# Mixture of experts: expert results added up by token in DRAM instead of stored, gathered and combined; four tiles fed by one-hot products; rows turned in mid-tile

## The reference, cut to what matters

```python
def _L0_ffn_ref(x, keys, w1, b1, w2, b2, rw, rb):
    # 512 tokens, D = 256, E = 16 experts, TOP_K = 4, F = 1024
    logits = -dist2 + jnp.einsum('bld,ed->ble', x, rw) + rb
    topv, topi = jax.lax.top_k(logits, TOP_K)
    w = jax.nn.softmax(topv, axis=-1)
    hidden = jax.nn.gelu(jnp.einsum('bld,efd->blef', x, w1) + b1, approximate=False)
    exp_out = jnp.einsum('blef,edf->bled', hidden, w2) + b2
    sel = jnp.take_along_axis(exp_out, topi[..., None], axis=2)
    return jnp.sum(w[..., None] * sel, axis=2)
...
x = x + _L0_ffn_ref(_layernorm(x, axis=-1), ...)
x = x + _L1_xattn_ref(_layernorm(x, axis=-1), ctx_1024, ctx_1024, mask, gamma, beta)
```

## Time and profile before

| | us |
|---|---|
| time, median of 3 runs | 872.52 |
| the runs | 868.11 to 873.1 |
| profiled execution, time | 865.21 |
| profiled execution, span | 863.3 |
| TensorE busy in the span | 723.3 (84%) |
| DVE busy | 501.6 (58%) |
| POOL busy | 313.4 (36%) |

### The profile page before, as it was taken

One profiled execution on the slowest core, in us unless ns is written; L12 is line 12 of the kernel. 1 busy time (PEld: TensorE's weight loads), 2 busy tenths in 40 slices (PEclk: granted clock), 3 DMA queues, 4 the chain that ended last, 5 costly groups with the idle time before them and its releaser, 6 DMA issues.

```text
span 863.3 us, 13603 instructions
## 1 busy us (share of the span) xinstructions
PE 723.3 (84%) x4928; PEld 550.0 (64%) x4928; DVE 501.6 (58%) x830; ACT 387.6 (45%) x729; POOL 313.4 (36%) x365
## 2 busy tenths in 40 slices
PE   5899999999999749699999999946976866665686
PEld 2677777777778538599999999932532322222575
DVE  4787778878778674011111111116666989997675
ACT  3766656656655323234444444412257643331441
POOL 6545425525445105540000000034103657753330
PEclk9999999999999958899999999987997999999898
DMA  7201101011002396898878888858210000000210
GB/s 313 75 2 49 32 19 49 0 49 49 0 0 98 131 412 253 287 354 305 311 293 310 304 310 309 320 205 347 98 55 0 0 1 0 0 0 0 74 36 25
DMA packets 19073, 118.18 MB, mean 137 GB/s; under 512 B 2144, under 2 KB 6768, under 8 KB 11728
## 3 DMA queue, kind: packets, MB, share of 16 engines
q1 hardware_dynamic: 16000, 109.28, 34.0%
q0 software_dynamic: 3024, 8.26, 2.5%
HBM read 106.79 MB, written 10.75 MB: 136 GB/s over the span
## 4 chain that ended last, share of the span: by engine, by line
PE 54%; DVE 24%; issue 8%; ACT 5%; POOL 4%; DMA 3%; DVEq 0%; SPq 0%; ACTq 0%; POOLq 0%; PEldq 0%
PE banks L1659 48%; DVE banks L1554 8%; PE banks L1721 4%; DVE k_stack L1154 3%; POOL x_slots L740 2%; ACT k_stack L850 1%; DVE negmax_raw L1206 1%; DVE hid_lo L1615 1%; DVE X L1622 1%; DVE shown L1562 1%; ACT ctx_hi L842 1%; DMA first<-in_first 1%; DVE conv L1279 1%; POOL y_rows L760 1%; DMA y_rows<-y_slots,slots 1%
## 5 line engine op out<-in xcount | busy, mean ns | idle before, releaser
L932 ACT ACTIVATE mid<-banks,later 128x128 f32<-128x128 f32 x248 | 91.1, 368 | 150.6 <-PE banks L1659 150.5
L1659 PEld LDWEIGHTS banks<-xT,raw 128*128 128x128 f32 x992 | 147.9, 192 | 12.2 <-issue 1.1
L1659 PE MATMUL banks<-xT,raw 128*128 128x128 f32 x992 | 151.6, 276 | 0.6 <-DVE xT L1389 0.6
L1659 PE MATMUL banks<-raw,mid 128*128 128x256 f32 x496 | 148.3, 382 | 0.0
L1395 DVE COPY y_tile<-banks 128x256 f32<-128x256 f32 x31 | 13.2, 424 | 197.6 <-PE banks L1659 197.6
L792 POOL TENSOR_TENSOR inject<-Bbc,drive 128x1024 f32<-128x1024 f32 x32 | 75.3, 2356 | 66.9 <-DVE banks L1554 29.9
L863 ACT ACTIVATE probs<-banks,negmax 128x1024 f32<-128x1024 f32 x64 | 71.5, 1117 | 58.4 <-DVE negmax L1209 57.7
L1659 PE MATMUL banks<-shown,table 128*128 128x512 f32 x128 | 66.4, 644 | 36.6 <-DVE shown L1562 29.9
L1206 DVE TENSOR_REDUCE negmax_raw<-banks 128x1 f32<-128x1024 f32 x64 | 78.0, 1218 | 20.5 <-PE banks L1659 20.5
L755 POOL DMA_DIRECT2D y_slots<-y_tile x31 | 17.0, 547 | 190.0 <-DVE y_tile L1395 189.9
L1659 PEld LDWEIGHTS banks<-raw,mid 128*128 128x128 f32 x496 | 75.8, 193 | 0.1
(11 more groups left out here) (285 smaller groups left out, 1399.4 us busy)
## 6 DMA issues: line engine op xcount, KB each, us to landing
raw<-in_w SPq DMA_DIRECT2D x31, 2048.0 KB, 8.7
ctx_raw<-in_ctxT SPq DMA_DIRECT2D x8, 1024.0 KB, 4.8
ctxT<-in_ctxT SPq DMA_DIRECT2D x4, 2048.0 KB, 8.4
ctxN<-in_ctxN SPq DMA_DIRECT2D x4, 2048.0 KB, 8.6
x_slots<-zero SPq DMA_DIRECT2D x1, 3968.0 KB, 12.5
y_slots<-y_tile POOLq DMA_DIRECT2D x31, 128.0 KB, 7.3
wf<-in_w SPq DMA_DIRECT2D x9, 384.0 KB, 3.0
later<-in_later SPq DMA_DIRECT2D x1, 2646.0 KB, 16.0
```

Of the source, the lines that this page charges most:

```text
L932: nc.scalar.activation(mid[n % HB][:], pb(UP_BANKS[n % 3])[:, 0:P], ACT.Gelu, bias=b1[:, bass.ds(at + u, 1)]).then_inc(gelu_done, 1)
L1659: return nc.tensor.matmul(o, lhsT, rhs, start=start, stop=stop)
```

## The change

What it removes: the stores to y_slots, the 16 gathers, the 16 combining steps, the product of gates and choices.

What it adds:
- A scattered row is 17 floats wider (XW = 273, 1,092 bytes): it carries the token's number, less an offset, and the token's 16 gates. The tile x_ext takes the place of xn for this layer. The gates are therefore computed inside place_rows, ahead of the slots.
- DVE reads from the arrived rows which token each row belongs to (tokens_of; unused rows go to a spare row behind the tokens) and its gate (gate_at). The first four tiles have their rows from the one-hot product, and for them a small load (hot_meta, 4 x 128 pieces of 68 bytes) fetches these 17 floats. In overflow tiles the gate is picked by the owner (owner_hot, over_gate). All of it happens on DVE at i = 3, between take_rows(4) and take_tile(3), after waits for all three pieces.
- take_tile multiplies by the gate as it evicts. Tiles 0 to 2 are evicted without it and weighed in place later (weigh_tile).
- GpSimd adds each y_tile by an indirect DMA with an add into x_added in DRAM, 640 rows of 256 floats, zeroed before. One add is issued when the one before has landed. take_tile(i) waits until add i - 4 has landed.
- After the last add SP loads x_added as four tiles of 128 KB, and DVE adds them to X. The layer norms then follow for all four tiles, and the attention starts after them. The two next context loads no longer wait for gathers.
- HOT is 4, so one more tile is fed by the one-hot product, and X_PIECES is (4, 8, 16, 31).
- turn_rows(i+1) comes in the middle of tile i, at its fifth unit, not at its start.

The core of the diff:

```diff
-HOT = 3
-X_PIECES = (HOT, HOT + 4, 16, TILES)
+HOT = 4
+X_PIECES = (HOT, HOT + 4, E0, TILES)
+XW, Z_PARTS = D + 1 + E0, 13
...
+            half = (TOK + P) * D // P // 2
+            sp.dma_start(x_added.rearrange("(p a) n -> p (a n)", p=P).rearrange("p (k n) -> p k n", k=2), over(zero[:, 0:half], 2, 1))\
                 .then_inc(zeroed, 16)
...
+                if k == 1:
+                    sp.dma_start(hot_meta[:], by_row[:, 0:HOT, D:XW]).then_inc(rows_loaded[1], 16)
+                sp.dma_start(x_rows[:, a - HOT:b - HOT, :], by_row[:, a:b, :]).then_inc(rows_loaded[k], 16)
...
-            sp.wait_ge(gathered[0], 16 * TOP0)
+            sp.wait_ge(y_added, 16 * TILES)
+            for t in range(TC):
+                sp.dma_start(x_sum[:, t, :], x_added[t * P:(t + 1) * P, :]).then_inc(gathered[t], 16)
             context_T(2)
             context_N(2)
-            sp.wait_ge(gathered[1], 16 * TOP0)
             context_T(3)
...
-            pool.wait_ge(zeroed, 16)
+            pool.wait_ge(zeroed, 32)
             pool.wait_ge(slots_ready, 1)
+            pool.wait_ge(gate_ready, 1)
...
-            def store_tile(i):
-                pool.wait_ge(y_taken, i + 1)
-                pool.dma_start(y_slots[i * P:(i + 1) * P, :], y_tile[i % YB][:]).then_inc(y_stored[i % YB], 16)
...
+            def add_rows(i):
+                if i < HOT - 1:
+                    pool.wait_ge(y_weighed, i + 1)
+                else:
+                    pool.wait_ge(y_taken, i + 1)
+                if i:
+                    pool.wait_ge(y_added, 16 * i)
+                nc.gpsimd.indirect_dma_start(x_added, bass.IndirectOffsetOnAxis(token[:, i:i + 1], 0), y_tile[i % YB][:], None,
+                                             compute_op=ALU.add).then_inc(y_added, 16)
...
+            order.step(nc.vector.tensor_reduce(here[:], earlier[:, 0:P], AX.X, ALU.add))
+            order.step(nc.vector.tensor_scalar(here[:], here[:], -1.0, float(P - 1), ALU.mult, ALU.add))
+            order.step(nc.vector.tensor_scalar(x_ext[:, :, D], inc[:, 0:TC], float(P), -float(TOK + P), ALU.mult, ALU.add))
+            order.mark(nc.vector.tensor_scalar(x_ext[:, :, D], x_ext[:, :, D], here[:], None, ALU.add))
...
                 one_hot(0)
+                gates()
...
+            def tokens_of(tiles, found):
+                order.step(nc.vector.tensor_scalar(spare[:, tiles], found, 0.0, here[:], ALU.is_equal, ALU.mult))
+                order.step(nc.vector.scalar_tensor_tensor(token_f[:, tiles], found, float(TOK), spare[:, tiles], ALU.add, ALU.add))
+                order.step(nc.vector.tensor_copy(token[:, tiles], token_f[:, tiles]))
+
+            def rows_arrive(k):
+                if k == 1:
+                    dve.wait_ge(rows_loaded[1], 32)
+                    tokens_of(slice(0, HOT), hot_meta[:, :, 0])
+                else:
+                    dve.wait_ge(rows_loaded[k], 16)
+                a, b = X_PIECES[k], X_PIECES[k + 1]
+                tokens_of(slice(a, b), x_rows[:, a - HOT:b - HOT, D])
+                if k == 2:
+                    order.step(nc.vector.tensor_tensor(owner_hot[:], owner_hot[:], x_rows[:, E0 - HOT:TILES - HOT, D + 1:XW], ALU.mult))
+                    order.step(nc.vector.tensor_reduce(over_gate[:], owner_hot[:], AX.X, ALU.add))
...
                 if i >= YB:
-                    dve.wait_ge(y_stored[i % YB], 16 * (i // YB))
+                    dve.wait_ge(y_added, 16 * (i - YB + 1))
...
-                if i == 0:
-                    gates()
+                if i == HOT - 1:
+                    for k in range(len(X_PIECES) - 1):
+                        rows_arrive(k)
+                    for j in range(HOT - 1):
+                        weigh_tile(j)
...
-            def combine(t):
-                dve.wait_ge(gathered[t], 16 * TOP0)
...
+            def arrive(t):
+                dve.wait_ge(gathered[t], 16)
+                order.step(nc.vector.tensor_tensor(X[:, t, :], X[:, t, :], x_sum[:, t, :], ALU.add))
+                norm_begin(4, t)
...
             arrive(0)
-            arrive(1)
+            for t in range(TC):
+                if t + 1 < TC:
+                    arrive(t + 1)
+                norm_tile(4, t)
...
-                if u == 0 and i + 1 < TILES:
+                if u == UNITS // 2 and i + 1 < TILES:
                     turn_rows(i + 1)
```

More of the change, by code:

```diff
@@ L250, in build @@
         place["common"], common_end = base, place["common"]
-        zero = sb("common", "zero", [P, TILES * D // 8])
+        zero = sb("common", "zero", [P, TILES * XW // Z_PARTS])
+        here = sb("common", "here", [P, 1])
         inc = sb("common", "inc", [P, P])
@@ L364, in build @@
         rows_loaded = [sem(f"rows_loaded{k}") for k in range(len(X_PIECES) - 1)]
-        y_stored = [sem(f"y_stored{k}") for k in range(YB)]
+        y_added, y_weighed = sem("y_added"), sem("y_weighed")
         gathered = [sem(f"gathered{t}") for t in range(TC)]
@@ L1379, in gates, with gate_at @@
                 order.step(nc.vector.reciprocal(best[:], best[:]))
-                nc.vector.tensor_tensor(gate[:], gate[:], over(best[:], E0, 2), ALU.mult).then_inc(gate_ready, 1)
-                dve.wait_ge(gate_ready, 1)
-                order.step(nc.vector.tensor_tensor(gate_of[:], chosen[:], over(gate[:], TOP0, 2), ALU.mult))
-                order.step(nc.vector.tensor_reduce(gate_top[:], gate_of[:], AX.X, ALU.add))
+                nc.vector.tensor_tensor(x_ext[:, :, D + 1:XW], gate[:], over(best[:], E0, 2), ALU.mult).then_inc(gate_ready, 1)
+            def tokens_of(tiles, found):
[13 more added lines that the diff above has]
+                    order.step(nc.vector.tensor_reduce(over_gate[:], owner_hot[:], AX.X, ALU.add))
+            def gate_at(i):
+                if i < HOT:
+                    return hot_meta[:, i, 1 + i:2 + i]
+                if i < E0:
+                    return x_rows[:, i - HOT, D + 1 + i:D + 2 + i]
+                return over_gate[:, i - E0:i - E0 + 1]
             def take_rows(i):
@@ L1417, in _ @@
                 take_tile(i)
-            def combine(t):
-                dve.wait_ge(gathered[t], 16 * TOP0)
-                for j in range(TOP0):
-                    order.step(nc.vector.scalar_tensor_tensor(X[:, t, :], y_rows[:, TOP0 * t + j, :], gate_top[:, t, j:j + 1],
-                                                              X[:, t, :], ALU.mult, ALU.add))
+            def arrive(t):
+                dve.wait_ge(gathered[t], 16)
+                order.step(nc.vector.tensor_tensor(X[:, t, :], X[:, t, :], x_sum[:, t, :], ALU.add))
+                norm_begin(4, t)
             def greatest(p):
@@ L1450, in normalise @@
                 order.mark(nc.vector.scalar_tensor_tensor(X[:, p, :], scaled, stat2[:, p, 3:4], X[:, p, :], ALU.mult, ALU.add))
-            def arrive(t):
-                combine(t)
-                norm_begin(4, t)
-                norm_tile(4, t)
-                dve.wait_ge(xn_ready, norm_of(4, t))
-                order.mark(nc.vector.tensor_tensor(X[:, t, :], X[:, t, :], part(rows, ROWS, "beta"), ALU.add))
             def leave(p):
@@ L1468, in _ @@
             arrive(0)
-            arrive(1)
+            for t in range(TC):
+                if t + 1 < TC:
+                    arrive(t + 1)
+                norm_tile(4, t)
+            dve.wait_ge(xn_ready, norm_of(4, TC - 1))
+            order.mark(nc.vector.tensor_tensor(X[:], X[:], over(part(rows, ROWS, "beta"), TC, 1), ALU.add))
+            dve.sem_inc(x_updated, 1)
             greatest(0)
-            arrive(2)
             greatest(1)
-            arrive(3)
-            dve.sem_inc(x_updated, 1)
             for p in range(TC):
@@ L1836, in turn_tokens @@
                 for c in range(DC):
[L1837 removed]
+                    of = x_ext if k == 3 else xn
+                    last = nc.tensor.transpose(pb(banks[p])[:, c * P:(c + 1) * P], of[:, p, c * P:(c + 1) * P], ident)
                 last.then_inc(early_turned, 1)
@@ L1926, in _ @@
                     for t in range(TC):
-                        last = nc.tensor.transpose(pb(3)[0:E0, t * P:(t + 1) * P], gate[:, t, :], ident)
+                        last = nc.tensor.transpose(pb(3)[0:E0, t * P:(t + 1) * P], x_ext[:, t, D + 1:XW], ident)
                     last.then_inc(gate_turned, 1)
```

81 lines of the change are left out of this document (42 added, 39 removed).

## The result

The changed kernel takes 882.47 us (median of 4 runs, 879.10 to 885.53); the kernel before, run beside it, 870.32 us (4 runs, 868.03 to 873.10). The ratio is 1.0143, 95% interval 1.0108 to 1.0178: slower, by 12 us. The profiled execution has a span of 877.3 us against 863.3.

What follows compares the result with a forecast made beforehand. TensorE was taken to bound the expert stage, 7.25 us a tile with no wait left. The last add at 584.5, against 582.9 for equal times, adds 1.6 us to the 872.5 median: 874, range 860 to 905.

Steps and rivals of the forecast that it cites:

- (b): Rival for the expert stage: adds do not lock to the loads but need 8.3 us throughout; 905 us, chance 0.25.
- (c): Rival: adds locked to the loads, but accumulation itself slow, 6 to 7 us alone; 886 to 890 us, chance 0.19.
- the gain from the hole: Ahead of the experts: TensorE's 8.0 us wait for x_rows goes, and about 1.2 us of low clock behind it.
- Part 3: Expert stage: one add per load, every 7.25 us, three tiles behind; four run alone at the end, sums in DRAM at 584.5.
- add 26: End of the expert stage: the last add beside a load, landing 7 us after the context load's issue, at 566.9.
- The 2.4 us of TensorE: Expert stage: 0.9 us for a late row copy and 1.5 us for the adds' lag reaching TensorE once.
- Rival (a): Adds catch up, each landing in 2.4 to 3.5 us, loads or not; 859 us, chance 0.13.
- Part 2: First tiles: x_rows wait removed, 1.6 us of products added; tile 3 ends near 369.1 instead of 375.63.
- Part 4: Hand-over to attention: four loads and adds replace gathers and combining; pair 0's transposes start 16.8 us after the last add.
- Part 1: Before the experts: three more small DVE instructions and settles on the path to the convolution cost 1.0 us.
- a DVE wait for the last piece near 370: Sign in the profile after: DVE waits for the last x_rows piece before evicting tile 3; it lands near 370.

Runs made afterwards that it cites:

- rows of 288: The changed kernel with each scattered row padded with zeros from 273 to 288 floats: 873.8 us, ratio 1.0051 to the kernel before.
- the kernel whose loads wait: The changed kernel, where from tile 5 each tile-end weight load waits until the add of the tile before is issued: 961.14 us, ratio 1.1018 to before.
- plain scatter: The changed kernel with plain scatters in place of the accumulating ones, still one behind the other: 865.0 us, ratio 0.9952 to the kernel before.
- rows turned first: The changed kernel with the next tile's rows turned in the first unit of each tile again: 875.9 us, ratio 1.0083 to the kernel before.
- before-with-four-tiles: The kernel before with four tiles by one-hot products and rows turned in mid-tile, without scatter-adds: 873.2 us, ratio 0.9994 to the kernel before.
- two sums: The changed kernel with even tiles added into one DRAM buffer and odd tiles into another: 868.86 us, ratio 0.9957 to the kernel before.

## Why the prediction was right, and where its sum went wrong

The forecast was 874 with 860 to 905 around it; 882.5 lies in it, on the slow side, where I had put most of what was left. But I had put it there for (b) and (c), and neither came; that the slow side was the right one is luck. The mechanisms of the chain and of the hand-over held. The largest term of the sum, the gain from the hole, did not.

**Part 3, the chain: right.** One add to each load, TensorE unbroken. Alone an add takes 3.6 to 3.7 us, against 3.5, and the cycle is 4.4, as summed. It runs three tiles behind, as said: in the steady stage an add goes out 22.5 us after the eviction of its tile, which is 3.1 tiles. One term was too small, the landing in company: 9.4 us behind the load's issue, not 8. The pace does not suffer, since the load still sets it, but the end does. I let the last add beside a load, add 26, land 7 us behind the issue of the context load, by a store that needed 6.0; it lands 9.3 behind it in the changed kernel (568.74 to 578.07) and in the one with rows of 288 (559.82 to 569.15), like the adds ahead of it. That is 2.3 us on the end. The 2.4 us of TensorE that I took for row copies and lag did not come in the changed kernel (there the lateness of everything had let x_rows land: 188.4 us from tile 3's load to tile 29's, as before), and 1.6 of them with rows of 288. Rival (a) is out: adds are not served at once beside loads. (c) is out by the 3.7. (b), the chain as the bound, came about only in the kernel whose loads wait. The Trainium skill (DMA: Bandwidth & Descriptors, Anatomy of one DMA) would have 2.3 us for these 128 KB; the plain scatter's 2.42 agrees, the accumulating one's 3.6 to 3.7 does not. The Trainium skill (Collectives: The Full Stack, Stop ④) describes an adding transfer as two reads and a write with the add free in between. No run here parts the adding from the second read and from the smaller packets; together they cost 1.25 us for each 128 KB.

**Part 2, the hole: its gain did not come.** I subtracted 8.0 us for the wait and 1.2 for the low clock behind it. On a chip without the loss that is right: with rows of 288 the load of tile 3's end goes out at 369.8 against my 369.1, that of tile 29's at 559.8 against 559.9, and the last add lands at 586.9 against 584.5. In the medians the two changed variants on chip 1 (rows of 288, rows turned first) are 5.6 and 7.7 us slower than before, where the forecast was 1.6. The one with rows turned first lost 3.5 us of TensorE when its first add took 12.2 us and held the eviction of tile 4, and 3.2 more behind that, where the granted clock was 0.50 for 6.8 us. The changed kernel itself was not run on chip 1 or 4.

On chips 2 and 3 the changed kernel is 10.3 and 10.1 us slower than before. If the kernel before has the loss there too, a part of it falls into the time in which TensorE would stand for x_rows anyway. Then the wait is a cover as much as a price, and taking it away lays the whole loss bare. Only a part can fall there, because a late tile 0 reaches x_rows too: SP issues the x_rows loads behind a 2 MB load that waits for the end of tile 0. Here are SP's timeline and the landing of the first piece, first in the kernel before, then before-with-four-tiles on chip 3, which has the same scatters:

```profile
340.07 0.33 SPq L446 DMA_DIRECT2D raw<-in_w  x1
352.84 1.60 SPq L476 DMA_DIRECT2D x_rows<-x_slots  x3
...
DMA to landing us min/median/max: 3.9/3.9/3.9
```
```profile
352.61 0.33 SPq L446 DMA_DIRECT2D raw<-in_w  x1
352.98 6.69 SPq L476 DMA_DIRECT2D x_rows<-x_slots  x3
...
DMA to landing us min/median/max: 10.2/10.2/10.2
```

The piece lands at 363.1 instead of 356.8; in the changed kernels with the loss at 361.0 to 365.3. An estimate from these rows: on such a chip the kernel before goes on 4 to 6 us late. The changed one goes on 10.5 to 15.0 late (tile 1 evicted at 361.7 in its first profile, at 364.0 and 366.2 on chips 2 and 3, against 351.2 with rows of 288). So the change costs at least 4.5 us more there than the 5.6 of chip 1, that is 10.1 or more; 10.1 and 10.3 were measured.

Three more results fit. The kernel before is 5.2 to 5.7 us slower in the medians on those two chips than on the others. Its executions under 870 us are 2 of 17 and 1 of 20 there, 22 of 31 and 9 of 13 on chips 1 and 4. And four tiles by products with mid-tile turning, worth 7.6 us by my sum, are worth 0.2 us there in the medians (0.9994). But no profile of the kernel before on such a chip was taken, so this step is argued, not shown.

**The hint that I passed over** was in the first table: the profiled execution took 865.2 us where the median was 872.5. I made the sum in the one and added the difference to the other, as if 7 us of spread lay outside the stretch that changes. In the only other profile of the kernel before, 8.4 us longer, 4.8 of them lie ahead of tile 3's end.

**Part 4, the hand-over: right.** 16.4 us from the last add to the transposes, against 16.8.

**Part 1: right in kind.** The setup moved the convolution by 0.6 us, and 1.0 was taken.

Together: in the changed kernel's profile 11.2 us late at tile 3, less the 2.4 that did not come, and 2.3 at add 26 are 11.1 of the 11.2 by which the last add misses 584.5.

The span grew by 14.0, 1.6 more than the 12.4 at the wf loads. That is no more than the scatter: from those loads to the end thirteen of the fourteen profiles (all but the one whose loads wait) take 232.8 to 238.1 us, with and without the change, and the first profile of before is the lowest.

The row that my text named as the thing to look for, a DVE wait for the last piece near 370, is absent from the changed kernel's profile: the loss made everything late, and x_rows was there at 371.9, ahead of its use at 377. Two profiles without the loss have it: 4.8 us, ended at 370.9, with rows turned first, and 1.2 us, ended at 372.2, with plain scatters.

## What to carry to other kernels

A wait that ends on a transfer can be taken off the time only if nothing else is spent beneath it; this case argues so and does not show it. Before its length is subtracted, look at a second execution, best the typical one, and ask what would be late without the wait. A chain of accumulating DMAs, each waiting for the last, locks to the loads beside it and leaves its whole lag as a tail; two sums, with four more loads and adds at the end to join them, broke the lock and made this kernel 14.8 us faster than the changed one on the same chip (13.9 and 17.1 with wider rows or rows turned first), and faster than the kernel before by 0.4 to 0.8%. In the changed kernel's steady stage the chain cost TensorE nothing (175.00 of 175 us); what the two sums gain is the tail.

## What the runs showed of the hardware

- An accumulating indirect DMA of 128 rows of 1 KB moves in 128 packets of 1,024 bytes, the first 2.1 us after issue; the plain scatter in 32 packets of 4,096, the first 1.5 us after issue. Alone they land in 3.5 to 3.9 us (the last four in each of five profiles) and 2.4 us, and GpSimd needs 1.54 and 0.96 us. Beside 2 MB loads both need 6.5 when they go out some 2.9 us behind the load; 9.4 from the load's issue.
- A load issued 1.0 us behind such an add still starts its packets 3.1 us ahead of it.
- In two of four groups of runs, each on a chip of its own, TensorE loses 10 us or more (10 or 11 gelus of 0.88 us are missing between 335 and 356 us) as it goes from the routing's short products to the dense stage. Its products finish late for 17 to 21 us, and most distances of the late gelus lie on steps of about 0.70 us: 2.12, 2.84, 3.55, 4.24, 4.94, 5.62, 6.30. One core ran. What does this stayed open, and so did whether it belongs to the chip or to the time of the group.
